# A two-layer memory, expert and attention kernel: regrouped waits in front of the expert layer, later expert groups, statistics ahead of a flag test, and another order of copies in the second layer

## The reference, cut to what matters

```python
x = L0_attn_x                                     # [1, 2048, 128]
xn = _layernorm(x)
x = x + memory(xn) + expert(xn)                   # first layer
xn = _layernorm(x)
x = x + attention(xn) + gated_network(xn)         # second layer

def memory(x):                                    # F = 64, D = 128
    k, q = phi(rmsnorm(x) @ Wk.T), phi(rmsnorm(x) @ Wq.T)
    v = rmsnorm(x) @ Wv.T
    for t in range(T):                            # a recurrence over 2048 tokens
        surprise = norm(v[t] - k[t] @ M)
        M = ln2(M + eta * surprise * outer(k[t], v[t]))
    return x + (q @ M) @ Wout.T                   # only the last M is used

def expert(x):                                    # the gate always picks expert 1
    return relu(x @ W1[1] + b1[1]) @ W2[1] + b2[1]

def attention(x):                                 # one head of 128, causal
    q, k, v = x @ wq, x @ wk, x @ wv              # half of q and k is rotated by position
    return softmax(mask(q @ k.T) / 128) @ v @ wo

def gated_network(x):                             # 128 -> 512 -> 512 -> 512 -> 128
    h = silu(lin(x, w1)) * lin(x, w2)
    return lin(gelu(lin(gelu(lin(h, h1)), h2)), w3)
```

## Time and profile before

| | us |
|---|---|
| median of three runs | 287.02 (286.99 to 287.1) |
| the profiled execution | 287.02 |
| its span | 285.1 |
| PE busy | 263.6 (92%) |
| DVE busy | 219.6 (77%) |
| ACT busy | 192.2 (67%) |
| POOL busy | 97.9 (34%) |

### The profile page before, as it was taken

How to read it: one execution, slowest core, us unless ns; L and a number is a source line. 1 busy time by engine, 2 the same in 40 slices (tenths; PEclk the granted TensorE clock), 3 DMA queues, 4 the chain that set the end, 5 groups by cost and what they waited for, 6 DMA issues and landing times.

```text
span 285.1 us, 5393 instructions
## 1 busy us (share of the span) xinstructions
PE 263.6 (92%) x1791; PEld 167.3 (59%) x1791; DVE 219.6 (77%) x745; ACT 192.2 (67%) x465; POOL 97.9 (34%) x121
## 2 busy tenths in 40 slices
PE   7999899796899969979999999999999999999993
PEld 2369854243456634746788777887696444444483
DVE  6978399998997589868999987788763666666674
ACT  1587487765445468777867689999773877777730
POOL 9210000000000025898885549998774000000000
PEclk9999999999799999999999999999999999999998
DMA  7700000000000065030000000000000000000005
GB/s 204 193 12 2 2 2 1 1 0 0 0 3 1 1 232 211 14 136 3 2 0 2 0 2 1 0 3 0 0 2 0 2 0 1 2 0 1 0 3 149
DMA packets 8287, 8.51 MB, mean 30 GB/s; under 512 B 1729, under 2 KB 7362, under 8 KB 7746
## 3 DMA queue, kind: packets, MB, share of 16 engines
q1 hardware_dynamic: 7826, 7.84, 8.7%
q10 hardware_dynamic: 432, 0.30, 0.4%
HBM read 7.09 MB, written 1.05 MB: 29 GB/s over the span
## 4 chain that ended last, share of the span: by engine, by line
PE 69%; DVE 19%; ACT 5%; issue 3%; DMA 2%; SPq 0%; DVEq 0%; ACTq 0%
PE PS L810 10%; PE PS L811 10%; PE PS L768 9%; PE PS L748 8%; PE PS L759 4%; PE PS L472 3%; PE PS L601 3%; PE PS L491 3%; PE PS L596 2%; DVE arena L1673 2%; PE PS L726 2%; PE PS L725 2%; DMA x<-L_attn_x 2%; PE PS L598 1%; PE PS L597 1%
## 5 line engine op out<-in xcount | busy, mean ns | idle before, releaser
L810 PE MATMUL PS<-arena 128*128 128x512 f16 x128 | 48.5, 379 | 0.6 <-issue 0.6
L811 PE MATMUL PS<-arena 128*128 128x512 f16 x128 | 48.5, 379 | 0.0
L1741 DVE TENSOR_TENSOR arena<-arena 128x512 f32<-128x512 f32 x32 | 22.2, 693 | 19.5 <-ACT arena L1184 19.5
L748 PE MATMUL PS<-arena 128*128 128x512 f32 (+3 forms) x80 | 31.9, 530 | 0.0
L1183 ACT ACTIVATE arena<-PS,arena 128x512 f32<-128x512 f32 x32 | 22.0, 688 | 13.2 <-PE PS L811 13.2
L1231 POOL CAST arena<-arena 128x512 f16<-128x512 f32 x2 | 1.2, 610 | 83.1 <-ACT x L1045 83.1
L1223 POOL TENSOR_TENSOR arena<-arena 128x256 f32<-128x256 f32 x32 | 21.5, 672 | 15.8 <-DVE arena L1680 13.8
L1157 ACT ACTIVATE arena<-PS,lnt 128x512 f32<-128x512 f32 (+3 forms) x40 | 24.9, 633 | 1.6 <-DVE lnt L1695 1.4
L1224 POOL TENSOR_TENSOR arena<-arena,small 128x256 f16<-128x256 f32 (+1 forms) x36 | 23.8, 660 | 2.8
L1688 DVE TENSOR_REDUCE mxb<-PS 128x1 f32<-128x512 f32 (+3 forms) x40 | 22.2, 602 | 1.6 <-PE PS L750 1.6
L1184 ACT ACTIVATE arena<-PS,arena 128x512 f16<-128x512 f32 x32 | 21.8, 681 | 0.0
(11 more groups left out here) (280 smaller groups left out, 635.1 us busy)
## 6 DMA issues: line engine op xcount, KB each, us to landing
arena<-h_T SPq DMA_DIRECT2D x2, 1024.0 KB, 5.7
x<-L_attn_x SPq DMA_DIRECT2D x4, 256.0 KB, 4.6
arena<-cos SPq DMA_DIRECT2D x1, 1024.0 KB, 4.7
arena<-sin SPq DMA_DIRECT2D x1, 1024.0 KB, 6.9
out<-arena SPq DMA_DIRECT2D x4, 256.0 KB, 2.3
arena<-w_T SPq DMA_DIRECT2D x3, 256.0 KB, 3.0
con<-shape_constants ACTq DMA_DIRECT2D x1, 192.0 KB, 3.3
w1e<-L_ffn_W SPq DMA_DIRECT2D x1, 128.0 KB
```

Source lines behind the costliest of these rows:

```text
L748: i = mm(PS[:, k, 0:cnt * P], qT1[:, t * P:(t + 1) * P], kT1[:, c * P:(c + cnt) * P], start=True, stop=not last)
L810: mm(bank(u % 8), wH[:, k, m * P:(m + 1) * P], sH[:, k, cols], start=(k == 0), stop=False)
L811: i = mm(bank(u % 8), wL[:, k, m * P:(m + 1) * P], sL[:, k, cols], start=False, stop=(k == HT4 - 1))
L1741: v.tensor_tensor(RP[m], FP[m], high, ALU.subtract).then_inc(rest_ready, 1)
```

## The change

1. PE: the fourth small product goes to bank 6 instead of bank 7, the eight warm-up matmuls before the hidden layer are gone, and all waits stand before the first of the eight hidden matmuls: for all four xT copies, all four `last_act` copies and q. ACT waits for the fourth product only before its own copy.
2. `EH_LATE` 5 to 6: two Relu copies before the scan loop instead of three. `EO_AT` (14, 17, 20, 24) to (14, 18, 21, 25), and the warm-ups of the late scan steps stand at steps 28 to 30 instead of 27 to 29.
3. Behind the scan: DVE computes `UW` and `WM` before `c0`; PE multiplies them before the shift; two warm-ups follow the shift instead of one following the products; the count matmul stands behind the first four of the sixteen memory products instead of before all.
4. DVE takes the statistics and variances of chunk 0 before the flag test (and again inside the general version, which needs them too) instead of after it.
5. ACT: `deviations(3)` before `transposed(1)` instead of after it.
6. ACT copies V1 chunks 0 and 1, DVE chunks 2 and 3, and DVE's wait for ACT's two; the high part of chunk 0 and the masks stand behind the last skip copies instead of in their midst.

```diff
-EH_LATE = 5
+EH_LATE = 6
...
-EO_AT = (14, 17, 20, 24)
+EO_AT = (14, 18, 21, 25)
...
-            mm(PS[0:L, 7, F + 2 * D:F + 2 * D + 1], lane[:, MM, :], con[:, C_ID + LAST:C_ID + LAST + 1], start=True, stop=True).then_inc(last_done, 1)
-
-            keep_warm(8, 6)
+            mm(PS[0:L, 6, 0:1], lane[:, MM, :], con[:, C_ID + LAST:C_ID + LAST + 1], start=True, stop=True).then_inc(last_done, 1)
+
             pe.wait_ge(moe_in, 64)
+            pe.wait_ge(xnt_act, 4)
+            pe.wait_ge(last_act, 4)
+            pe.wait_ge(qphi_act, 2)
             for h in range(2):
                 for ch in range(4):
-                    if h == 0:
-                        pe.wait_ge(xnt_act, ch + 1)
-                    if (h, ch) == (0, 0):
-                        pe.wait_ge(qphi_act, 2)
-                    if (h, ch) == (0, 3):
-                        pe.wait_ge(last_act, 4)
...
-                elif EO_AT[-1] + 2 < j < L - 2:
+                elif EO_AT[-1] + 2 < j < L - 1:
                     keep_warm(3, 4)
...
-            pe.wait_ge(c0_ready, 1)
-            mm(PS[0:W - 1, 5, HALF:2 * HALF], con[0:W, C_ID + 1:C_ID + W], c0, start=True, stop=True).then_inc(shift_done, 1)
             pe.wait_ge(uw_ready, 2)
             pe.wait_ge(wvo_act, 1)
             mm(PS[0:F, 7, 0:D], UW, VW, start=True, stop=False)
             mm(PS[0:F, 7, 0:D], WM, WSUM, start=False, stop=True).then_inc(mw_done, 1)
-            keep_warm(1, 4)
-
-            pe.wait_ge(agree_ready, 1)
-            mm(PS[0:1, 5, 1:2], agree[0:W - 1, :], con[0:W - 1, C_ONES:C_ONES + 1], start=True, stop=True).then_inc(count_done, 1)
+
+            pe.wait_ge(c0_ready, 1)
+            mm(PS[0:W - 1, 5, HALF:2 * HALF], con[0:W, C_ID + 1:C_ID + W], c0, start=True, stop=True).then_inc(shift_done, 1)
+            keep_warm(2, 4)
+
+            def agreed():
+
+                pe.wait_ge(agree_ready, 1)
+                mm(PS[0:1, 5, 1:2], agree[0:W - 1, :], con[0:W - 1, C_ONES:C_ONES + 1], start=True, stop=True).then_inc(count_done, 1)
...
-            for two in range(2):
-                memory_output(two, 0, 4)
+            memory_output(0, 0, 2)
+            agreed()
+            memory_output(0, 2, 4)
+            memory_output(1, 0, 4)
...
-            act.wait_ge(last_done, 2)
+            act.wait_ge(last_done, 1)
...
-            f(negm, PS[0:L, 7, F + 2 * D:F + 2 * D + 1], ACT.Copy, scale=-1.0).then_inc(last_act, 1)
+            act.wait_ge(last_done, 2)
+            f(negm, PS[0:L, 6, 0:1], ACT.Copy, scale=-1.0).then_inc(last_act, 1)
...
             normed(2)
+            deviations(3)
             transposed(1)
-            deviations(3)
             normed(3)
...
-                if c == 2:
-                    act.wait_ge(xt2_act, 1)
-                    high(0)
-                    f(ident_b, ident, ACT.Copy).then_inc(mask_act, 1)
-                    f(causal_b, con[:, C_CAUSAL:C_CAUSAL + P], ACT.Copy).then_inc(mask_act, 1)
-            act.wait_ge(v1_act, 2)
-            for c in range(2, 4):
+            act.wait_ge(xt2_act, 4)
+            high(0)
+            f(ident_b, ident, ACT.Copy).then_inc(mask_act, 1)
+            f(causal_b, con[:, C_CAUSAL:C_CAUSAL + P], ACT.Copy).then_inc(mask_act, 1)
+            for c in range(2):
...
-            first_variances()
...
+            dve.wait_ge(ao_done, 1)
+            first_variances(o).then_inc(var2_ready, 1)
             general_path(dve, general)
...
-            for c in range(2):
+            dve.wait_ge(v1_act, 2)
+            for c in range(2, 4):
```

25 lines of the change are left out of this document (15 added, 10 removed).

## The result

The changed kernel takes 291.09 us (median; 290.62 to 291.32), the kernel before 287.06 (286.99 to 289.05) beside it: a ratio of 1.0106, with a 95% interval of 1.0069 to 1.0143. The prediction was 288.5 us, 286.9 to 289.2. The sign is right, the size is not: the profiled execution of the changed kernel takes 290.06 us (span 288.2, mean granted clock 0.982), that is 3.04 more than the 287.02 of the kernel before, where 1.45 was forecast. The other 1.0 between the medians has to do with which executions are met: on one chip single executions of the kernel before lie up to 4.7 us apart (286.90 to 291.55), and those of the changed kernel, 39 of them with a median of 290.49, lie between 289.19 and 292.76, but for one at 295.61.

A forecast was written before the change was run, and what follows sets the result against it. PE was taken to bound the loop, a chain of waits across engines its start. Terms 0.45 + 0.25 + 0.75 = 1.45 on 287.02 gave 288.5 us, range 286.9 to 289.2.

The forecast's parts named there:

- What bounds the kernel: PE fills the loop from 140 to 216 us and hands on any starting delay whole; a chain of waits sets its start.
- Part 1: Hidden layer and scan start, 36 to 50 us: later expert burst at half clock, +0.45 us, bounds 0 to 0.7.
- Part 2: EO_AT and the late scan steps' warm-ups: expert groups and warm-ups still fit before the last scan, cost 0.
- Part 3: Flag and first variances, 95 to 101 us: test behind the variances, +0.25 us at normed(0), bounds +0.05 to +0.55.
- The relay's -0.2: Behind the scan: UW and WM start earlier and the shift no longer precedes them, so memory output starts 0.2 us earlier.
- The -0.3 at the statistics: First block complete at about 98.8, so DVE's first statistics start there instead of 99.14 us.
- the dear end: After the flag branch: DVE loses the full 0.45 us, perhaps a fetch stall, putting the reciprocal at 101.65.
- Rival (b): Flag test: DVE's sequencer runs ahead under the statistics, -0.3 instead of +0.25, total 287.9 us; chance 0.07.
- Parts 4 and 5: Second layer's ACT order and V1 copies: late chunk 1 projection delays the loop start +0.75 us, bounds 0.5 to 1.0.
- (a): Expert burst: clock does not fall or is nearly back, cost 0 to 0.1, total 288.0 to 288.1 us; chance 0.18.
- (c): Whole change: none of it is on the path, several chains being near, total 287.0 us; chance 0.10.
- (d): Second layer: early DVE statistics spare ACT its wait in deviations(3), total 286.2 us, faster; chance 0.15.

The follow-up runs named there:

- p1_bridged: Kernel before with gathered waits and EH_LATE 6, PE's pause before the expert burst filled by 18 warm-up matmuls: median 289.76 us, lowest 287.00.
- p1_gathered: Kernel before with gathered waits, EH_LATE 6, negm by bank 6 and the eight warm-ups gone, nothing else: median 289.18 us, lowest 288.40.
- after_again: The changed kernel itself, unaltered, run again beside the kernel before on one chip: median 290.82 us, lowest 290.31.
- p5_v1: Kernel before with only the V1 copies exchanged between ACT and DVE, high(0) and the two small copies behind the last skip copy: median 289.53 us, lowest 287.29.
- p3_flag: Kernel before with only DVE's first statistics and variances moved ahead of the flag test: median 290.81 us, lowest and profiled 287.86.
- p3_relay: Kernel before with UW and WM ahead of c0, the shift behind WM's matmul, the count within the memory output, flag test unmoved: median 292.25 us, lowest 288.12.
- after_no1: Changed kernel with the old expert-burst waits, eight warm-ups, negm in bank 7 and EH_LATE 5 restored: median 291.43 us, lowest 289.11.
- after_bridged: Changed kernel with 18 warm-ups ahead of the gathered waits and negm back in bank 7: median 292.16 us, lowest and profiled 288.88.
- p4_dev3: Kernel before with only ACT's deviations(3) moved ahead of transposed(1): median 290.04 us, lowest and profiled 287.83.
- fill_gap: Kernel before with 11 warm-up matmuls in PE's 2.65 us pause before the first expert group: median 287.71 us, lowest 287.12.
- fill_more: Kernel before with 11 warm-ups in PE's pause near 70 us and three more behind scan step 30: median 287.77 us, lowest 286.84.

## Why the prediction was right or wrong

**What bounds the kernel** held: PE's rows in the loop are the same, and delays before it come out at the end, less 0.34. That the loop hands on "whole, whatever delay" was wrong by this small amount.

**Part 1** is the step that failed most: forecast +0.45 with an upper bound of 0.7, measured +1.42. The mechanism was right, and p1_bridged shows the fall of the clock to be the whole of it; its size was too small at two places. At step 1 it is +1.04 and not +0.5, because ACT's second copy ended at 49.66 (48.97 + 0.69) and not at 49.0: PE started at 45.18 and not at 44.9, and ACT could begin its two copies 2.15 and 3.79 us after that (47.33, 48.97), where 1.8 and 3.3 had been taken. At step 4 another 0.43 is added. The low stretch was taken to end "about 2.9 us after PE resumed" as in the earlier trace rows, which gave about 48; it ended at 49.5, 4.3 us after PE resumed (5.4 in p1_gathered, 5.1 in after_again). One row of another gap had been carried over as if it were a constant. The far matmuls behind the burst thus began at 54.26 and not near 53.4, and at step 3 DVE had to wait for the first, where the forecast had "about nothing to spare". The bound of 0.7 was meant to hold all of this, a burst slow throughout.

**Part 2**, cost 0, is right for the profiled execution. What was missed is what the earlier trace rows say beside that: 0.53 us is all that PE has to spare at the last scan, so that a longer low stretch goes straight into the time. By p5_v1 and p1_bridged, this is where the single executions part.

**Part 3**: forecast +0.25 with an upper bound of 0.55 at `normed(0)`, measured +0.83. The relay's -0.2 is right (-0.24). The -0.3 at the statistics was -0.05: the forecast let them start at 98.85, 1.25 us behind the memory output's first matmul; measured are 1.51 us (99.00 to 100.51), which puts them at 99.09, less the shift. Without the count matmul in between, p3_flag shows 1.20 us (98.01 to 99.21). Then the load began at 100.5 and not at 100.2, and after the branch there were 0.5 us more. The forecast had named them, "the 0.45 being what DVE lost at 99.14 after its branch if that, not PE, held it", and had taken the value in the middle; p3_relay shows that the dear end was the true one. The Trainium skill, "Runtime: NRT & Kernel Launch", section "Instruction fetch mechanics", holds that a taken branch may stall for a fetch: the 0.52 us between the branch's end and DVE's next instruction in five profiles (the changed kernel twice, p3_flag, after_no1, after_bridged) agree with that, but no run separates the fetch from other causes. Rival (b), the sequencer running ahead, fell: the load starts at 101.9, when the last variance is under way.

**Parts 4 and 5**: forecast +0.75 (0.5 to 1.0), measured +1.15, or +0.83 without the 0.3 that goes with part 1 and whose cause stays open. The chain was right link by link for `deviations(3)`: projection of chunk 1 +1.4 (p4_dev3: +1.51), chunk 2 +0.8 (+0.98), V1 +0.65 (+0.80), first tanh +0.75 (+0.80). The V1 exchange, which the forecast wrote into the chain, is worth 0.03.

**Rivals.** (a), no fall of the clock, and (c), nothing on the path, fell with the profile. (d), faster, fell: the statistics lacked not 1.0 us but more, since they came later. The range failed because each of the three parts came out above its own upper bound (1.42 against 0.7, 0.83 against 0.55, 1.15 against 1.0), and because a fourth source, where the low stretches fall in an execution, was in no term: single executions of the kernel before run from 287 to 291, and with the pause filled they end at 288.3 to 288.6.

## What to carry to other kernels

A pause of PE is not free where the next burst is on the path: read the length of the low stretch, not only that there is one, and give its end a bound from more than one gap. Before moving a test of a flag, measure from the flag's write to the engine's next instruction (1.53 us here) and see whether that interval is already the one that holds the engine; it costs the same wherever it stands uncovered. When an engine fills its time up to a relay with 0.5 us to spare, start its work earlier: putting the first expert group into the pause, or warm-ups, brought the median from 289.8 or 288.8 to 287.7 or 287.8, by removing the long executions; the lowest stayed where they were. Judge a change by the lowest, the median and the profiled events together: for this change the lowest say 2.2 and 3.3 us on two occasions, the medians 4.0 and 2.0, the profiled execution 3.0.

## What the runs showed of the hardware

The length of a low-clock stretch (granted clock 0.50) differs between executions of the same place: 3.4, 10 and 13.8 us from 70 to 72 us on in kernels whose work up to there is alike (the kernel before, p5_v1, p1_bridged); after PE's pause of 4.6 us it was 6.8 us in two profiles of kernels with part 1 (42.7 to 49.5, 43.8 to 50.6). It also comes without a long pause: at 96 to 103 us in fill_gap and fill_more, where PE's matmuls are short. The mean granted clock of an execution tells most of its time: the kernel before takes 286.9 to 287.4 at 0.991 to 0.993, mostly 289.5 to 290.1 at 0.973 to 0.980, and mostly 290.5 to 291.5 at 0.961 to 0.976.

The branch on DVE's sequencer was followed by 0.5 us in which DVE did nothing, in all five profiles read for it, on top of 0.95 us for load, register instructions and branch.
